# A four-layer spectral convolution whose mode mix is taken apart by image halves and placed inside the channel passes

## What is computed

```
h = gconv1x1(concat(x, coordinates), fc0_w, fc0_b)          # 40 channels (4 groups of 10), per image
for i in range(4):
    xf  = rfft2(h)                                          # kept: 24 rows kx, 12 columns ky
    lo  = einsum('bgixy,gioxy->bgoxy', xf[:, :, :, :12, :12],  w1[i])
    hi  = einsum('bgixy,gioxy->bgoxy', xf[:, :, :, -12:, :12], w2[i])
    h   = irfft2(lo and hi in place, zero elsewhere) + gconv1x1(h, w_w[i], w_b[i])
    h   = gswish(h)                                         # not after the last layer
out = fc2(gswish(fc1(h)))
```

## Time and profile before

| | us |
|---|---|
| median of 3 runs | 3454.14 |
| lowest and highest | 3449.07, 3454.84 |
| the profiled execution | 3450.26 |
| its span, first to last instruction | 3448.4 |
| PE, DVE, ACT, POOL busy in it | 2794.9, 1863.9, 1404.4, 705.8 |

### The profile page before, as it was taken

The page is one execution under the profiler, slowest core; times in us unless marked ns, Lnnn a source line. Parts: engine busy times, 40 slices in busy tenths (PEclk is TensorE's granted clock), DMA queues, the critical chain, the costliest instruction groups (busy, mean ns, idle before and its releaser), DMA issues. The chain is left out here.

```text
span 3448.4 us, 44291 instructions
## 1 busy us (share of the span) xinstructions
PE 2794.9 (81%) x16948; PEld 2101.2 (61%) x16948; DVE 1863.9 (54%) x2412; ACT 1404.4 (41%) x2331; POOL 705.8 (20%) x653
## 2 busy tenths in 40 slices
PE   0699997969666199569996799769996699999658
PEld 0344441126344199569995799669995687887535
DVE  6888773327534411254554445354454578878643
ACT  1877773422122122153333333253333466666322
POOL 3988500012110000000000000000000044444310
PEclk9999998989788599889998999979998899999879
DMA  8200005569424455958767677657776624332134
GB/s 212 60 24 0 24 17 142 155 154 198 126 89 143 89 130 134 219 157 190 194 156 205 146 184 195 164 164 178 182 189 176 126 52 91 56 61 51 62 89 94
DMA packets 344104, 437.92 MB, mean 127 GB/s; under 512 B 260535, under 2 KB 302135, under 8 KB 317519
## 3 DMA queue, kind: packets, MB, share of 16 engines
q1 hardware_dynamic: 343428, 430.41, 51.8%
q0 software_dynamic: 496, 5.01, 0.4%
HBM read 258.59 MB, written 168.58 MB: 124 GB/s over the span
## 5 line engine op out<-in xcount | busy, mean ns | idle before, releaser
L1026 DVE STREAM_TRANSPOSE spec_chan<-spec_form_in 128x1024 f32<-128x1024 f32 x256 | 492.1, 1946 | 62.2 <-PE fno_pz L1242 62.2
L1328 ACT ACTIVATE fno_act<-fno_pz 128x320 f32<-128x320 f32 x512 | 224.0, 437 | 616.1 <-PE fno_pz L1242 616.1
L1412 DVE COPY fno_wfreq<-fno_pw 128x240 f32<-128x240 f32 x256 | 97.8, 395 | 513.7 <-PE fno_pw L1270 511.8
L1217 POOL TENSOR_SCALAR fno_minus<-fno_both 96x960 f32<-96x960 f32 x32 | 83.4, 2607 | 1376.8 <-DVE fno_both L1420 1376.8
L1242 PEld LDWEIGHTS fno_pz<-spec_cols,spec_chan 128*128 128x128 f32 x3072 | 348.2, 192 | 12.3 <-issue 9.5
L1242 PE MATMUL fno_pz<-spec_cols,spec_chan 128*128 128x96 f32 x3072 | 350.0, 275 | 2.0 <-ACT spec_cols L1336 2.0
L1293 PE MATMUL fno_pz<-fno_act,fno_wt 128*40 128x64 f32 x2304 | 204.5, 263 | 149.5 <-DMA fno_act<-scratch_modes 107.1
L1270 PE MATMUL fno_pw<-fno_fw,fno_act 128*128 128x96 f32 x2560 | 303.4, 277 | 14.4 <-DVE fno_wfreq L1412 8.6
L1546 POOL TENSOR_TENSOR head_hact_lo<-head_hact,head_hact_hi 128x512 fp32r<-128x512 f32 x128 | 227.9, 1783 | 400.4 <-DVE head_hact_hi L1693 400.4
L1270 PEld LDWEIGHTS fno_pw<-fno_fw,fno_act 128*128 128x128 f32 x2560 | 291.4, 192 | 26.9 <-DVE fno_wfreq L1412 15.4
L1293 PEld LDWEIGHTS fno_pz<-fno_act,fno_wt 128*40 128x40 f32 x2304 | 197.6, 139 | 158.8 <-issue 146.0
(11 more groups left out here) (158 smaller groups left out, 4628.4 us busy)
## 6 DMA issues: line engine op xcount, KB each, us to landing
scratch_form<-fno_act SPq DMA_DIRECT2D x32, 2560.0 KB, 17.2
spec_form_in<-scratch_form SPq DMA_DIRECT2D x64, 1024.0 KB
fno_act<-scratch_modes SPq DMA_DIRECT2D x128, 180.0 KB
nca_win<-scratch_xnp SPq DMA_DIRECT2D x66, 329.7 KB
fno_coef<-scratch_mixed SPq DMA_DIRECT2D x48, 360.0 KB, 10.8
spec_form_in<-scratch_form SPq DMA_DIRECT2D x32, 512.0 KB
fno_wt<-table_mix_w SPq DMA_DIRECT2D x32, 450.0 KB, 11.1
gn_x<-scratch_x SPq DMA_DIRECT2D x12, 1024.0 KB
```

The lines of the kernel that those rows point to most:

```text
L1026: return nc.vector.transpose(chan[:, to * TR * PIX:(to + 1) * TR * PIX].rearrange("p (h q w) -> p h q w", h=TR, q=4), src)
L1328: nc.scalar.activation(act_b[:, n % 2, :, 4 * t:4 * t + 4], z, ACT.Silu if layer else ACT.Copy).then_inc(a_out, 1)
```

## The change

The units are numbered n = 0 to 31 over all layers. Four successive units are one half of the images; there are 8 halves q. The mix of half q runs inside the passes of units 4(q+1)+1 and 4(q+1)+2, which belong to the other half: one mix tile m behind each of the pointwise tiles t = 3 to 14, so 12 tiles a unit and 24 a half. A tile is now one row kx with all 12 ky and the 16 images of the half: 12 matmuls of 32 columns, into `pj`, whose two banks it shares with the inverse rows. The last half's mix stands alone behind the last unit. Further:

- `act_b` has one buffer; the modes have buffers of their own (`xm`, XB = 3 chunks of XC = 2 rows), the results three buffers of one tile each (`om`, OB = 3), stored by one DMA a tile.
- The weights are loaded once for each half, so twice a layer.
- Modes are collected over four units in `both` and `minus` and stored together (`begin_mix`, `store_modes`), and coefficients are loaded for two units at a time.
- `mix_out` of ACT (odd tiles) stands behind `activate` of the same t; DVE's (even tiles) has its first three each behind one of the unit's last four turns.
- The fill of `cols` is done by POOL (first half) and ACT (second half) at the end of a layer's last unit, in place of the DMA.
- SP's order in a unit: begin_mix or the mix's loads and stores first, then the form store, the read-back, the coefficients.
- The memset of `wt` (and one of `xm`) moves behind those of `form_in`.

The diff, cut to its core:

```diff
-XC = 3
+XC = 2
+XB, OB = 3, 3
+PER, MIX_AT = NX // 2, 3
+FH = B * KY // 2
...
-        act_b = ph.sb("act", [128, 2, CS, H])
+        act_b = ph.sb("act", [128, CS, H])
...
+        def mixed_in(n):
+            q = n // 4 - 1
+            return range(q * NX + PER * (n % 4 - 1), q * NX + PER * (n % 4)) if q >= 0 and n % 4 in (1, 2) else range(0)
+        last_mix = range((SIDES - 1) * NX, SIDES * NX)
...
+                def load_modes(c):
+                    if c >= XB:
+                        sp.wait_ge(mix_done, (c - XB + 1) * XC)
+                    x, f = c % CHUNKS * XC, c // CHUNKS % 2 * FH
+                    for half in range(2):
+                        for ri in range(2):
+                            sp.dma_start(xm[half * CH:half * CH + CH, c % XB, :, ri, :],
+                                         modes[1 - half + ri, x:x + XC, :, f:f + FH].rearrange("x c f -> c x f")).then_inc(x_in[c % XB], 16)
...
+                def begin_mix(q):
+                    for c in range(XB):
+                        load_weights(q * CHUNKS + c)
+                    store_modes(q)
+                    sp.wait_ge(both_out, 64 * (q + 1))
+                    for c in range(XB):
+                        load_modes(q * CHUNKS + c)
+                def store_mixed(m):
+                    sp.wait_ge(out_s if m % 2 else out_v, m // 2 + 1)
+                    f = m // NX % 2 * 2 * FH
+                    sp.dma_start(mixed[:, m % NX, :, f:f + 2 * FH].rearrange("r c f -> c r f"), om[:, m % OB, :, :]).then_inc(stored[m % OB], 16)
+                def feed_mix(m):
+                    if m % XC == XC - 1 and m // XC % CHUNKS + XB < CHUNKS:
+                        load_modes(m // XC + XB)
+                        load_weights(m // XC + XB)
+                    if m % NX:
+                        store_mixed(m - 1)
...
+                for n in range(ALL):
+                    if n % 4 == 0 and n:
+                        begin_mix(n // 4 - 1)
+                    for m in mixed_in(n):
+                        feed_mix(m)
+                    sp.wait_ge(a_out, (n + 1) * NZ)
+                    if n:
+                        sp.wait_ge(act_stored, 16 * n)
+                    sp.dma_start(form[layer % 2, u], act_b[:, :, :].rearrange("p c h -> p (c h)")).then_inc(act_stored, 16)
...
+                    if u == UNITS - 1:
+                        pool.wait_ge(z_done, (n + 1) * NZ)
+                        nc.gpsimd.tensor_copy(cols[:, 0:COLS // 2].rearrange("p (h c) -> p h c", c=CS), wide(wsm[:, layer, :], H // 2, 1)).then_inc(fill_pool, 1)
...
+                def mix(m):
+                    pj_free(("mix", m))
+                    for y in range(KY):
+                        mm = nc.tensor.matmul(pj[0:CH, pj_at["mix", m] % 2, y * 32:(y + 1) * 32], wt[:, c % XB, m % XC * KY + y, :],
+                                              rows[:, :, :, y, :], start=y == 0, stop=True, skip_group_check=True)
+                    mm.then_inc(mix_done, 1)
+                for n in range(ALL):
+                    for t in range(NZ):
+                        if t == 2 and n:
+                            forward_rows(n - 1)
+                        pointwise(n, t)
+                        if len(mixed_in(n)) and MIX_AT <= t < MIX_AT + PER:
+                            mix(mixed_in(n)[t - MIX_AT])
+                    if UNITS <= n + 1 < ALL:
+                        inverse_rows(n + 1 - UNITS)
+                    forward_cols(n)
+                forward_rows(ALL - 1)
+                for m in last_mix:
+                    mix(m)
...
+                def mix_out(m):
+                    act.wait_ge(mix_done, m + 1)
+                    if m >= OB:
+                        act.wait_ge(stored[m % OB], 16 * (m // OB))
+                    for ri, v, part, sign in PARTS:
+                        op = nc.scalar.activation(om_tile(m, ri, v), acc_tile(m, part), ACT.Copy,
+                                                  scale=rates[0:CH, 2 if sign > 0 else 3, 1, layer:layer + 1])
+                    op.then_inc(out_s, 1)
...
+                    if n % UNITS == UNITS - 1:
+                        nc.scalar.activation(cols[:, COLS // 2:COLS].rearrange("p (h c) -> p h c", c=CS), wide(wsm[:, n // UNITS, :], H // 2, 1), ACT.Copy).then_inc(fill_act, 1)
+                        act.wait_ge(fill_act, n // UNITS + 1)
+                        act.wait_ge(fill_pool, n // UNITS + 1)
```

More of the change, by code:

```diff
@@ L1084, in om @@
[L1084 to L1094, removed]
+        blank, blank_half, mix_blank = (ph.sem(n) for n in ("blank", "blank_half", "mix_blank"))
@@ L1206, in _ @@
+                begin_mix(SIDES - 1)
+                for m in last_mix:
+                    feed_mix(m)
+                for b in range(OB):
+                    sp.wait_ge(stored[b], 16 * NX // OB * SIDES)
+                sp.wait_ge(act_stored, 16 * ALL)
                 sp.wait_ge(iw_in, 64)
@@ new lines, in _ @@
+                for n in range(ALL):
+                    for t in range(NZ):
+                        activate(n, t)
+                        if len(mixed_in(n)) and MIX_AT <= t < MIX_AT + PER and (t - MIX_AT) % 2:
+                            mix_out(mixed_in(n)[t - MIX_AT])
+                    if n % UNITS == UNITS - 1:
+                        act.wait_ge(scaled, LAYERS)
+                        act.wait_ge(z_done, (n + 1) * NZ)
+                        nc.scalar.activation(cols[:, COLS // 2:COLS].rearrange("p (h c) -> p h c", c=CS), wide(wsm[:, n // UNITS, :], H // 2, 1), ACT.Copy).then_inc(fill_act, 1)
+                        act.wait_ge(fill_act, n // UNITS + 1)
+                        act.wait_ge(fill_pool, n // UNITS + 1)
+                    if UNITS <= n + 1 < ALL:
+                        cols_out(n + 1 - UNITS)
@@ L1359, in _ @@
+                for m in last_mix[1::2]:
+                    mix_out(m)
             @block.vector
             def _(dve):
-                nc.vector.memset(wt[64:128, :, :, :], 0.0).then_inc(wt_blank, 1)
                 for b in range(2):
@@ new lines, in _ @@
+                for n in range(ALL):
+                    if n:
+                        row_spectra(n - 1)
+                    outs = mixed_in(n)[0::2]
+                    for e in range(4):
+                        if n >= UNITS:
+                            turn(n, 4 + e)
+                        if len(outs) and e < 3:
+                            mix_out(outs[e])
+                    for m in outs[3:]:
+                        mix_out(m)
+                    for t in range(NW):
+                        column_spectra(n, t)
+                        if UNITS <= n + 1 < ALL and t % 2:
+                            turn(n + 1, t // 2)
@@ L1455, in unit_loads @@
+                row_spectra(ALL - 1)
+                for m in last_mix[0::2]:
+                    mix_out(m)
 def unit_loads(n):
```

346 lines of the change are left out of this document (134 added, 212 removed).

## The result

The changed kernel is **slower**, by 1.6%: 3510.2 us median (3507.9 to 3512.5, four runs) against 3454.5 (3449.1 to 3456.4), ratio 1.0163, 95% interval 1.0145 to 1.0182. I had forecast 3413. The profiled execution's span is 3509.0 us, 60.6 more than that of before.

The account below looks back on a forecast made before the run. PE was taken to bound the kernel, busy 81%, with 413 us lying in mixes, fill, drain and coefficient waits. New costs of 383 gave -30, with gains -37, so 3413 us; the range was 3335 to 3515.

Parts of the forecast that it names:

- The price of a moved tile: PE time of one mix tile of 24 records at 40 ns: 1.0 us, bounds 1.0 and 1.95.
- Rival 1: Mix tile price goes by record, 1.95 us a tile, so PE paces the pass: 3486 us, slower; chance 0.15.
- The milder form: Each mix matmul costs the sequencer about 62 ns: 1.5 us a tile, 20.5 a pass, 3434 us, inside the range.
- The three buffers: Main term: output buffers waiting for stores pace mixing passes, 2.3 us a tile, mean 19 us a pass, 266 in 14.
- the test that I had set: Output waits under 2 us a pass would make the main term wrong even if the total fits.
- the collision: Read-back and coefficient pair, 8 us late, run into the next pass's first tiles: 3.5 us in six passes, 21.
- Rival 3: Clock falls in mixing passes because PE is sparsely busy; 30% of passes affected, +40 us: 3453, no change; chance 0.10.
- Rival 2: Queue fuller than assumed in mixing passes: store landing 7.5 us, slower loads, +106 us: 3519, slower; chance 0.17.
- Tail: Last half's mix behind the last unit: 20 us gap plus 24 tiles at 2.2, 52; together 72 us.
- Filling cols: POOL and ACT copies at three layer ends cost 5.8 us each, 17 in all; bounds 1 and 7 each.
- other waits: Late forward columns in units 5 and 6, and layer 1's first turn waiting for its tables: 5 us.
- signs of failure: Profile signs listed as wrong, among them records 80 ns apart, mode or weight waits in a pass, PEclk 0.8 in passes.

Follow-up runs that it names:

- e11: Changed kernel with the stores of mixed tiles issued by GpSimd from its own queue; 3473.8 us, ratio 1.0048 to the kernel before.
- e4: Changed kernel with PE repeating eight records of 480 columns behind the sixth mix tile of each half's first mixing unit; 3470.1 us, ratio 1.0043.
- e12: Changed kernel with mixed stores from GpSimd, four output buffers, odd pairs' coefficients in eight pieces behind tiles 1 to 8, wide burst in unit 5 alone; 3393.8 us.
- e3: Changed kernel with 19 of the 20 columns of the odd pairs' coefficients not loaded; 3455.1 us, ratio 0.9991.
- e10: Changed kernel with early even-tile stores, four output buffers, coefficients in pieces, wide burst in first mixing units, unit 7's coefficients before tables and read-back; 3402.7 us.
- e9: Changed kernel with even-tile stores ahead of next loads, four output buffers, odd pairs' coefficients in eight pieces behind tiles 3 to 10, no burst; 3413.3 us.
- e6: Changed kernel with PE repeating 48 records of 32 columns behind the sixth mix tile of each half's first mixing unit; 3572.4 us, ratio 1.0337.
- e1: Changed kernel with form store and read-back issued before the wait for stored modes, mode loads after them; 3538.4 us, ratio 1.0241.

## Why the prediction was wrong, point by point

- **The price of a moved tile was right.** 24 records and the change of operand take 1.07 us (24 in 1.14 with the last one's tail, 40 ns apart); I took 1.0. That the row tile beside it would rise from 0.89 to 1.06 I had not counted. Rival 1 (1.95) is out, and with it, for this operand, the rule of the Trainium skill, "SBUF — State Buffer", Door 1, as I applied it: if runs of two numbers cost nothing, 32 columns could not take half the time of 64. The milder form, "TensorE: Matmul & The Clock Gate" in the Trainium skill, Back-to-back issue gap (about 62 ns a matmul with hardware decode off), would have given 1.5; the trace doesn't show it.
- **The three buffers don't pace an undisturbed unit.** Their term gave 18 to 20 us a unit. Second units cost 14.9 beyond a plain one (51.3 in most runs): twelve steps of 2.13 us in place of 0.89, PE's own time. Over 14 passes the whole term would have been 209, not 266. By the test that I had set, output waits under 2 us a pass, the main term was wrong. The mechanism exists only where stores start and land late, and then at once, not spread over the tiles: I took a landing of 5 us everywhere, and in e11's trace it is 6.6 to 9.9 for the first six stores of unit 9 and mostly 2.5 to 4 in unit 10. The term was 57 us too high and hid that much of what follows.
- **The failed step** is the collision: "run into the next pass's first tiles: 3.5 us in six passes, 21". It was a stall of 10.8 us in each of six passes, 65, because I counted the bytes ahead and not that SP stands at each issue into the full queue. So the first mixed stores start 7 us late, and then they land in 9 to 10 us, not 5.
- **What the sum lacked** is the clock behind the stall, and it is the larger part. A second unit takes 51.3 us; 75.5 less 51.3 less 10.8 leaves 13.4 in each of six, 80 in all: 11.0 from the step times and 2.1 from the inverse rows. I had the clock as a rival of its own, for sparse tiles; it needs the stall to fall, and that joins rivals 2 and 3 into one case. Rival 3's own price was too low: 30% of 168 tiles at 1.1 to 1.5 us more are 55 to 76 us, not 40. Rival 2's 3519 is near the result by size, by another path: landing 9.4 us once, not 7.5 throughout. That the result lies just inside my range is owed to its width and not to the sum, which had the direction wrong.
- Unit 5 has the same two causes with another trigger: in layer 0 the form store is late, and ACT's activates wait for it. I said 2 us; PE stood 5.9, and then the clock fell: 41.1 beyond a plain unit, where a second unit has 15. The store itself lands in 9.1 us, about the 10 that I took. e4's burst took 8.3 off this unit.
- Unit 7: a wait of 11.1 us for the first coefficients, which stand behind two tables and a read-back. I had not counted it; 14.0 in all, where 5.8 stood for filling cols.
- Tail 77.9 against 72: PE stood 23.1 us before the first tile, after 3.5 of forward rows, where I took 20; the 24 tiles took 50.8, as forecast (52).
- Filling cols cost 1.7 and 3.3 us at two layer ends, not 5.8 (6.9 less 1.8 would have been 5.1). The first pointwise came 4.0 us earlier, about as forecast for the memset, but that start ranged from 1187.0 to 1197.5 in the other runs, so the gain isn't shown. Behind the last mix 4.0 us are gone, where I took 2 for the last stores; what saved them wasn't looked at.

By terms: the units with mixing 385 for 289 (with their collisions), tail +6, unit 7 +8, the other fills -7, and none of the 5 for other waits seen by itself: 482 for 383. What I listed as signs of failure, PEclk low in the passes, is what came. A gain of this kind did exist: e12 is 59 us below before.

Open: why the clock survived stalls of 1.6 and 2.0 us (e3) and fell behind others of 1.4 (e12) and 1.6 (e3); and whether the 22 us ahead of the tail can be shortened, which wasn't tried, and unit 7, beyond e10.

## What to carry to other kernels

A wait costs more than its length where narrow matmuls follow it: look up the granted clock behind each wait, multiply the tiles up to the work that raises the clock again by the difference, and add it to the same case as the wait. When work is spread beside other work, place every small store that frees a buffer where its issue doesn't stand behind large loads, from another engine if there is one, and cut large loads into pieces between them. Don't expect it to land sooner for that while the DMA engines are full, and don't take its landing from a median over all stages; do all of it, since each cut alone leaves a stall long enough to lose the clock. Where a stall can't be avoided, a few wide matmuls behind it can pay for themselves.

## What the runs showed of the hardware

- Behind a stall, tiles of 32 and 96 columns in turn ran at 1.2 GHz for 26.5 us with PE 26.46 busy (after, unit 9); without one, the same ran 25 us at 2.4 (e9). Eight records of 480 columns brought the clock back within their 4.6 us (e4), 48 of 32 in 7.9 us didn't (e6), and a row of 96-column records did within 5 us (after, unit 5).
- The clock was lost behind waits of 1.4, 1.6 and 1.9 us (e12 unit 17, e3 units 21 and 14) and kept behind waits of 1.6 and 2.0 (e3 units 25 and 26).
- At full clock a record of 32 columns read in runs of two numbers costs 40 ns, one of 64 costs 80: there the cost goes by columns. At half clock 64 cost 107 and 32 cost 67, more than half.
- With the DMA engines full, a 0.12 MB store landed 9.4 us after its issue from SP (after, unit 9) and 9.7 to 10.9 us from GpSimd (e11, the first store of the six first units). SP took 7.4 us to issue two coefficient loads (after) and 13.7 for twelve mode loads (e1) into a full queue; four mode loads took 1.4 with room (after, 1557.38).
